# A decoder layer with a mixture of experts: each expert's input rows are transposed in 32x32 blocks by VectorE instead of by TensorE

## The reference, cut to what matters

```python
xf = x.reshape(t, d)                                # t = 3584 tokens, d = 512
probs = softmax(xf @ Wr);  eidx = argmax(probs)     # one expert per token
xe = xf[dispatch]                                   # 8 experts x 448 slots x 512
h  = maximum(einsum('ecd,edf->ecf', xe, W1), 0)     # 512 -> 2048
ye = einsum('ecf,efd->ecd', h, W2)                  # 2048 -> 512
y  = zeros.at[dispatch].add(ye * p_tok)
x  = layernorm(x + y)
```

## Time and profile before

| | us |
|---|---|
| median of 3 runs (2598.73 to 2604.12) | 2603.05 |
| the profiled execution | 2615.71 |
| its span, first to last instruction | 2613.9 |
| busy: TensorE, VectorE, ScalarE, GpSimd | 2438.4, 2081.8, 1749.5, 1786.7 |
| first expert's first matmul of L1683 starts at | 1932.26 |
| last expert's rows_back starts at | 2595.4 |

### The profile page before, as it was taken

The page is one execution under the profiler, slowest core; times in us unless marked ns, Lnnn a source line. Parts: engine busy times, 40 slices in busy tenths (PEclk is TensorE's granted clock), DMA queues, the critical chain, the costliest instruction groups (busy, mean ns, idle before and its releaser), DMA issues.

```text
span 2613.9 us, 33259 instructions
## 1 busy us (share of the span) xinstructions
PE 2438.4 (93%) x11291; PEld 2070.1 (79%) x11291; DVE 2081.8 (80%) x2288; ACT 1749.5 (67%) x4011; POOL 1786.7 (68%) x1045
## 2 busy tenths in 40 slices
PE   7698999999999999999999999997879999999997
PEld 6686787878788787878878787785658989989896
DVE  4899999999999999999999999998833445444452
ACT  5677888888888888888888888887633333333331
POOL 1989999999999999999999999999600101001100
PEclk9899999999999999999999999998979999999998
DMA  6041202212020221202122020211233333234320
GB/s 205 15 132 67 85 15 85 71 36 89 13 91 15 85 75 33 89 18 85 33 75 79 22 92 15 78 50 50 85 127 120 125 125 125 100 128 139 132 75 18
DMA packets 90901, 202.62 MB, mean 78 GB/s; under 512 B 7997, under 2 KB 16843, under 8 KB 90751
## 3 DMA queue, kind: packets, MB, share of 16 engines
q1 hardware_dynamic: 81534, 179.21, 21.1%
q0 software_dynamic: 5120, 14.21, 1.7%
q10 hardware_dynamic: 4096, 7.34, 0.9%
HBM read 171.32 MB, written 29.95 MB: 77 GB/s over the span
## 4 chain that ended last, share of the span: by engine, by line
PE 54%; POOL 25%; DVE 8%; issue 5%; ACT 4%; DMA 3%; SPq 0%; POOLq 0%; DVEq 0%; ACTq 0%
POOL arena L1003 14%; PE work L1683 12%; PE y L1664 11%; PE ring L1683 11%; PE work L1442 7%; PE work L1471 5%; DVE ring L1313 4%; POOL arena L1008 4%; POOL arena L1014 3%; DMA arena<-bc_rows 2%; PE work L1486 2%; ACT ring L858 1%; POOL arena L936 1%; POOL arena L934 1%; POOL arena L932 1%
## 5 line engine op out<-in xcount | busy, mean ns | idle before, releaser
L1003 POOL TENSOR_TENSOR arena<-arena 128x896 f32<-128x896 f32 x512 | 1056.7, 2090 | 20.6 <-PE y L1664 10.1
L858 ACT ACTIVATE ring<-arena,small 128x224 f32<-128x224 f32 x2048 | 794.4, 436 | 138.3 <-DVE arena L1322 106.1
L1313 DVE TENSOR_TENSOR_SCAN ring<-ring,arena 128x896 f32<-128x896 f32 x400 | 809.4, 2024 | 59.3 <-POOL arena L1003 33.5
L1664 PE MATMUL y<-arena,cst_sb 128*128 128x224 f32 x3584 | 775.5, 369 | 75.7 <-POOL arena L1014 57.8
L1664 PEld LDWEIGHTS y<-arena,cst_sb 128*128 128x128 f32 x3584 | 699.5, 199 | 147.4 <-POOL arena L1014 64.1
L1027 POOL DMA_INDIRECT out<-res,ids x32 | 48.9, 1529 | 639.4 <-DVE mst L1368 540.2
L1322 DVE TENSOR_TENSOR arena<-ring,arena 128x896 f32<-128x896 f32 x400 | 433.3, 1083 | 6.0
L1442 PE MATMUL work<-arena 128*128 128x224 f32 x2000 | 428.1, 372 | 6.7 <-DVE arena L1093 6.2
L1442 PEld LDWEIGHTS work<-arena 128*128 128x128 f32 x2000 | 400.9, 203 | 19.1 <-issue 6.8
L1383 DVE SCALAR_TENSOR_TENSOR hidden_lo<-work,hidden_hi 128x448 fp32r<-128x448 f32 x128 | 79.9, 625 | 349.7 <-ACT hidden_hi L902 349.7
L902 ACT ACTIVATE hidden_hi<-work 128x448 fp32r<-128x448 f32 x128 | 69.8, 546 | 374.0 <-PE work L1683 374.0
(11 more groups left out here) (211 smaller groups left out, 3300.3 us busy)
## 6 DMA issues: line engine op xcount, KB each, us to landing
weights<-in_w SPq DMA_DIRECT2D x64, 1024.0 KB, 7.3
arena<-bc_rows SPq DMA_DIRECT2D x128, 448.0 KB, 4.4
arena<-in_ctx SPq DMA_DIRECT2D x16, 896.0 KB, 5.6
expert_rows<-x2e SPq DMA_DIRECT2D x1, 7224.0 KB, 30.1
arena<-in_xT SPq DMA_DIRECT2D x16, 448.0 KB, 6.5
arena<-in_x SPq DMA_DIRECT2D x16, 448.0 KB, 3.7
out<-arena ACTq DMA_DIRECT2D x32, 224.0 KB, 2.3
xrow<-expert_rows SPq DMA_DIRECT2D x7, 903.0 KB, 11.8
```

The costliest lines, as they stand in the source:

```text
L858: last = nc.scalar.activation(decays[s % 2][:, i * L:(i + 1) * L], delta[:, k, :], ACT.Exp, scale=a_neg[:, n:n + 1])
L1003: nc.gpsimd.tensor_tensor(u[:, u_of(b, s)], dx[:, k:k + 1, :].to_broadcast([P, QN, L]), bc[:, 0, q * QN:(q + 1) * QN, :], ALU.mult).then_i ...
L1313: nc.vector.tensor_tensor_scan(states, h, u_flat[:, u_of(b, s), :], 0.0, ALU.mult, ALU.add).then_inc(scan_done, 1)
L1664: last = nc.tensor.matmul(o, ident, u[:, u_of(b, s), i, :], start=False, stop=(q == Q - 1 and i == QN - 1), skip_group_check=True)
```

## The change

The rows are loaded a second time, four DMAs per expert, to a new tile `xblk`: partition k*32+t holds, for each of 14 blocks b of 32 rows, the 128 floats k*128 to k*128+127 of row b*32+t. VectorE's transpose turns every 32x32 block in its place: chunk c takes columns c*32 to c*32+31 of each. A partition k*32+j of chunk c then is feature k*128+c*32+j, and the host puts W1's rows in that order. The chunks go to `oT`, which is free between rows_back and copy_results; this is done behind f = 8 to 11 of the expert before. At the change of expert ScalarE and VectorE make hi and lo chunk by chunk from `oT` and wait for the last lo before copy_results overwrites it; TensorE waits chunk by chunk within hidden(e, 0). `xrow` is still loaded, for the residual and the tokens' numbers. `w_dt` moves to the arena to make room. Cut to its core:

```diff
-            ("x_res", 2 * D), ... ("ctx", 2 * DCTX),
+            ("x_res", 2 * D), ... ("ctx", 2 * DCTX), ("w_dt", DI),
-        w_dt = sb("w_dt_sb", [R + 1, DI])
+        w_dt = flat("w_dt")[0:R + 1]
+        TB = CAP // 32
+        xblk = moe("rows_in_blocks", TB * P).rearrange("p (b d) -> p b d", b=TB)
@@ SP
+            def load_blocks(e):
+                rows = xe_dram.rearrange("(e b t) d -> e t b d", b=TB, t=32)[e]
+                for k in range(DC):
+                    sp.dma_start(xblk[k * 32:(k + 1) * 32], rows[:, :, k * P:(k + 1) * P]).then_inc(blk_loaded, 16)
             def load_expert(e, par):
+                sp.wait_ge(t_turned, e * DC)
+                load_blocks(e)
...
-            for m in range(CM):
-                sp.dma_start(xrow[0][0:H, m], xe_dram[m * H:(m + 1) * H]).then_inc(first_rows[m], 16)
+            load_blocks(0)
+            load_rows(0, 0)
@@ ACT
             def take_rows(e):
-                for m in range(CM):
-                    act.wait_ge(t_full, e * CM + (m + 1))
-                    nc.scalar.activation(r32(xe_hi[:, :, m * H:(m + 1) * H]), turned_in(e, m)...)
+                for c in range(DC):
+                    act.wait_ge(t_turned, e * DC + (c + 1))
+                    nc.scalar.activation(r32(xe_hi[:, c, :]), oT[:, c, :], ACT.Copy).then_inc(t_hi, 1)
             def expert(e, last=False):
                 if later:
+                    act.wait_ge(t_split, e * DC + DC)
                     copy_results(e - 1)
@@ DVE
+            def turn_rows(e, c):
+                if c == 0:
+                    dve.wait_ge(blk_loaded, e * (16 * DC) + 16 * DC)
+                nc.vector.transpose(oT[:, c, :].rearrange("p (b t) -> p b t", t=32), xblk[:, :, c * 32:(c + 1) * 32]).then_inc(t_turned, 1)
             def take_rows(e, par):
+                for c in range(DC):
+                    dve.wait_ge(t_hi, e * DC + (c + 1))
+                    nc.vector.tensor_tensor(r32(xe_lo[:, c, :]), oT[:, c, :], xe_hi[:, c, :], ALU.subtract).then_inc(t_split, 1)
                 if not isinstance(e, int) or e >= 2:
                     for k in range(2):
                         dve.wait_ge(out_scattered[k], e * (8 * CM) - 8 * CM)
...
-                for m in range(CM):
-                    dve.wait_ge(t_hi, e * CM + (m + 1))
-                    nc.vector.tensor_tensor(r32(xe_lo[:, :, cols]), turned_in(e, m)..., xe_hi[:, :, cols], ALU.subtract)
             def expert(e, par, last=False):
                 if later:
+                    dve.wait_ge(t_split, e * DC + DC)
                     copy_results(e - 1)
...
+                    if FK - 8 <= f < FK - 8 + DC and not last:
+                        turn_rows(e + 1, f - FK + 8)
...
+            for c in range(DC):
+                turn_rows(0, c)
             take_rows(0, 0)
@@ PE
             def hidden(e, f):
-                three_passes(h_bank[f % 2][:, 0:CAP], [(...) for c in range(DC)], True, True).then_inc(h_full, 1)
+                for c in range(DC):
+                    if f == 0:
+                        pe.wait_ge(t_split, e * DC + (c + 1))
+                    last = three_passes(h_bank[f % 2][:, 0:CAP], [(... c ...)], c == 0, c == DC - 1)
+                last.then_inc(h_full, 1)
             def rows_back(e, m):
-                if m >= 2:
+                if m >= 2 or not isinstance(e, int) or e >= 1:
                     pe.wait_ge(o_free, e * CM + (m - 1))
-            def take_row(e, par, m):
...
             def expert(e, par):
-                for m in range(CM):
-                    take_row(e, par, m)
-                    if later and m % 2:
-                        results(e - 1, FK - 2 + m // 2)
-                pe.wait_ge(t_split, e * CM + CM)
+                if later:
+                    results(e - 1, FK - 2)
+                    results(e - 1, FK - 1)
                 hidden(e, 0)
@@ host
-        "w1": g["L0_ffn_W1"],
+        "w1": g["L0_ffn_W1"].reshape(E, D // P, D // P, 32, -1).swapaxes(1, 2).reshape(E, D, -1),
```

More of the change, by code:

```diff
@@ L79, in build_decoder @@
             ("x_res", 2 * D), ("r", 2 * D), ("hx", 2 * D), ("hT", 2 * DC * H), ("ctx", 2 * DCTX),
+            ("w_dt", DI),
         ):
@@ L255, in build_decoder @@
         last_clear = sem("last_rows_cleared")
-        first_rows = [sem(f"first_rows{m}") for m in range(CM)]
         wait_kept = sem("wait_kept")
@@ L1336, in take_rows @@
                     apart(dve)
-                if isinstance(e, int) and e == 0:
-                    for m in range(CM):
-                        dve.wait_ge(first_rows[m], 16)
-                else:
-                    dve.wait_ge(row_loaded[par], (e - par) * 8 + 16 * par)
-                nc.vector.tensor_copy(ids[:, par, :], xrow[par][0:H, :, D + 1]).then_inc(ids_ready, 1)
-                for m in range(CM):
-                    dve.wait_ge(t_hi, e * CM + (m + 1))
-                    cols = slice(m * H, (m + 1) * H)
-                    nc.vector.tensor_tensor(r32(xe_lo[:, :, cols]), turned_in(e, m)[:, 0:DC * H].rearrange("p (c n) -> p c n", c=DC),
-                                            xe_hi[:, :, cols], ALU.subtract).then_inc(t_split, 1)
+                dve.wait_ge(row_loaded[par], (e - par) * 8 + 16)
+                nc.vector.tensor_copy(ids[:, par, :], xrow[par][0:H, :, D + 1]).then_inc(ids_ready, 1)
             def copy_results(e):
@@ L1693, in hidden @@
                     pe.wait_ge(hid_split, e * FK + (f - 1))
-                three_passes(h_bank[f % 2][:, 0:CAP], [(w1_hi[g][:, c, cols], w1_lo[g][:, c, cols], xe_hi[:, c, :], xe_lo[:, c, :])
-                                                       for c in range(DC)], True, True).then_inc(h_full, 1)
+                for c in range(DC):
+                    if f == 0:
+                        pe.wait_ge(t_split, e * DC + (c + 1))
+                    last = three_passes(h_bank[f % 2][:, 0:CAP], [(w1_hi[g][:, c, cols], w1_lo[g][:, c, cols], xe_hi[:, c, :], xe_lo[:, c, :])],
+                                        c == 0, c == DC - 1)
+                last.then_inc(h_full, 1)
             def results(e, f):
@@ L1722, in rows_back @@
                 last.then_inc(b_full, 1)
-            def take_row(e, par, m):
-                if isinstance(e, int) and e == 0:
-                    pe.wait_ge(first_rows[m], 16)
-                else:
-                    pe.wait_ge(row_loaded[par], (e - par) * 8 + 16 * par)
-                if m >= 2 and (not isinstance(e, int) or e >= 1):
-                    pe.wait_ge(t_split, e * CM + (m - 1))
-                elif not isinstance(e, int) or e >= 2:
-                    pe.wait_ge(o_free, e * CM + (m + 3 - 2 * CM))
-                for c in range(DC):
-                    last = nc.tensor.transpose(turned_in(e, m)[:, c * H:(c + 1) * H], xrow[par][0:H, m, c * P:(c + 1) * P], ident[0:H, 0:H])
-                last.then_inc(t_full, 1)
             def expert(e, par):
                 later = not isinstance(e, int) or e > 0
-                for m in range(CM):
-                    take_row(e, par, m)
-                    if later and m % 2:
-                        results(e - 1, FK - 2 + m // 2)
-                pe.wait_ge(t_split, e * CM + CM)
+                if later:
+                    results(e - 1, FK - 2)
+                    results(e - 1, FK - 1)
                 hidden(e, 0)
```

11 lines of the change are left out of this document (4 added, 7 removed).

## The result

The changed kernel takes 2585.09 us (median of 4 executions, 2582.86 to 2590.66) where the kernel before takes 2603.59 (4, 2598.73 to 2605.84). The medians differ by 18.5 us. The measured ratio, which is not the quotient of these two medians, is 0.9943 with a 95% interval of 0.9929 to 0.9957, that is 11 to 18.5 us less: a small gain, but clear of the 0.2% that can be told from no change. Forecast were 17 us less and 2586.

What follows compares the result with a forecast made beforehand. TensorE alone was taken to set the pace from 1932.2 us on. Terms -19.5 + 0.5 + 1.0 + 0.65 + 0.5 = -16.9 us, taken from 2603.05, gave 2586 us, range 2578 to 2596.

Steps and rivals of the forecast that it cites:

- TensorE's 16 transposes and their wait at a change go.: At the seven changes of expert: 53.8 us shrink to 14 plain rounds, 19.5 us less.
- What TensorE would wait for instead.: At each change: VectorE's chain readies each `xe_lo` some 0.6 us early; waits inside hidden(0) cost 0.5 us in all.
- Rival B: At each change: VectorE late, TensorE waits about 1 us, +7 us; chance 0.12, plus 0.04 with the whole gain gone.
- Four VectorE transposes.: Per expert, behind f = 8 to 11: 0.6 us each, in VectorE's idle time, cost 0.
- Rival C: VectorE's transpose several times dearer: slower than before from 4.1 us each, 2629 us at 5 us; chance 0.05.
- The first expert, where nothing covers.: At the first expert's start: rows land later, +1.0 us, and landing to first matmul takes longer, +0.65 us.
- TensorE's clock there.: At the first expert's first rounds: the half-clock stretch may last longer without earlier transposes, +0.5 us, near to nothing.
- The rest: Doubled loads of 0.9 MB per expert, `w_dt`'s place and W1's order: cost 0.
- Rival A: Within experts: TensorE's pace shifts between 2.43 and 2.48 us per round; 3.8 us less to 5.2 more; chance 0.20.

Runs made afterwards that it cites:

- one turn for all experts: The kernel before, with only the first expert's rows turned and split and experts 1 to 7 computing with those: 2586.24 us, ratio 0.9936.
- the warmed kernel: The changed kernel plus 32 matmuls on TensorE, results overwritten, while the first expert's rows arrive: 2584.58 us, ratio 0.9932; run again 2582.8 us.

## Why the prediction was right

The sign, the size and the term that carries it were right, and the time of 2585.09 lies 0.9 us from the forecast. By its steps:

- **"TensorE's 16 transposes and their wait at a change go."** Forecast -19.5, measured -19.7. That one turn for all experts gives the same 4.87 us per change shows that nothing of the detour is left on TensorE's path.
- **"What TensorE would wait for instead."** The chain in VectorE was right to 0.2 us; its 0.5 us of waits did not occur, because each `xe_lo` was 0.7 us early or more; the text itself had 0.6. Rival B (VectorE late at each change) is out; transposes made twice didn't bring it either, since they lie behind f = 8 to 11 and not in that chain.
- **"Four VectorE transposes."** 0.6 us was taken between 0.575 and 1.01; the row says 633 ns, and four in a row take 2.23, so each follows the last after 0.53. Rival C (4.1 us and more) is out. By the Trainium skill's page Vector Engine (DVE) Microarchitecture Reference, 3.8, the reshape front-end, a transpose sustains one element per cycle per lane. The trace agrees in so far as a transpose costs no more than a plain operation of its shape: four take 2.23 us, four `xe_lo` 2.22.
- **"The first expert, where nothing covers."** Landing +0.8 for +1.0, tail +0.4 for +0.65. The 512 B pieces do arrive later than 2064 B ones of the same bytes: the last lands 5.6 to 6.5 us after the first issue in seven traces with row loads, and 6.8 to 7.0 in five with block loads (8.1 in the sixth, the warmed kernel, whose issues took longer). By the Trainium skill's page DMA: Bandwidth & Descriptors, How a descriptor splits into AXI transactions, the estimate was 0.5 for that; the trace has 0.3 more, and no run tells the piece size from the other traffic of the moment, or from the fact that a block load writes 32 partitions where a row load writes 112. The forecast of 1934.4 for the first matmul, 10.7 us after the first issue, came out as 9.8; it did not follow from the text's own +1.65 either, which gives 1933.9, 10.2 after.
- **"TensorE's clock there."** Forecast +0.5, measured -0.3: the sign was wrong, and the difference is within what these rounds vary between the traces.
- **"The rest", at nothing.** Right for the loads (686.3 against 686.3) and for `w_dt` (0.9994). Wrong in leaving out the instruction stream: taking 68 instructions out ahead of the loop and some 67 within it put the loop where it is fetched anew in every pass, 2.8 us in this execution and 3.5 in the next. The trace of before had the signs, 7 packets of queue 8 in the first pass and then none, but the prediction did not look at instruction queues.
- **Rival A, the pace**, with a chance of 0.20 half each way, happened on its fast side: experts 2, 4 and 6 run at 2.43 and only expert 0 at 2.48, 3.8 us less. "I see no cause" still holds. With the transposes left in, 50 slow rounds went when only `w_dt`'s address changed, and 28 with 64 idle increments, so the breaks that the edit takes away are not the cause alone. But they have a part in it, it seems: expert 2 is slow in all four traces that keep TensorE's transposes at every change, and experts 2 to 7 are fast in all nine that do not. So the loss of two breaks, which the rival named, fits expert 2; experts 4 and 6 were luck as far as can be told.

The two terms put at nothing have opposite signs: without the pace's gain the changed kernel would stand near 2589, still within 2578 to 2596, and without the loop's loss near 2582. That the time came within 1 us of the forecast is luck; that it came within the range is not. The range's upper end was added up without the 7 us that the text itself allowed for waits on `xe_lo`, and that did not matter.

**Still open.** What decides the pace of the matmul stream between 2.43 and 2.48 us for 12: it is drawn anew at breaks in the stream and comes out the same for one program in two executions (27 and 28 slow rounds), but no rule fits all kernels here. Which places let the loop be kept is fitted and not tested; shown is that 64 instructions toggle it. Nor is it known why single executions of 4904, 10734 and (of before's kernel) 3124 us occur.

## What to carry to other kernels

When one engine alone sets the pace, count what each stage asks of it beyond its own work, and draw the chain on the idle engine that would take the work over, from the last thing it must do first to the moment the busy engine asks: here that gave 19.5 us where 19.7 came. Where two profiled executions differ by more than the edit, align both at the first instruction of the changed stage and account from there. If a long hardware loop runs on the busy engine, look at the packets of the instruction queue in its later passes: if they go on, write the loop out or shift it, and see whether the waits marked "issue" at its turns go.

## What the runs showed of the hardware

- A loop of some 1,700 TensorE instructions can be kept, or fetched again in each pass (15 packets of 16 KB in 310 us against none), by a shift of 64 instructions, in either direction. Fetching as such costs nothing: the loop written out is fetched throughout (13 packets in that stretch) and has no wait. The turn back costs 1.1 to 2.0 us each time where TensorE has nothing else to wait for.
- Matmuls of 448 columns at full clock have two steady paces in these traces, 12 in 2.43 or in 2.48 us.
- VectorE's 32x32 transpose of 128x448 fp32 costs 633 ns, and 0.53 from one to the next.
- After 8.25 us of matmuls and a pause of 2.65 us, TensorE began again at 1.2 GHz; with shorter pauses of 0.4 and 0.7 us among its fillers it was at 2.4 GHz.
- One execution ran all matmuls at little over half pace (a 128x224 one 615 ns for 366) while the trace gives the clock as 1.00: the granted clock does not tell every slowdown.
